# Unread TensorE products in front of five waits of each turn of a four-layer kernel

## The chip, the cores and the metric

The kernel runs on one core of one Trainium2 chip. The metric is the device time of one execution in microseconds, as the median of several runs. A profile of one execution comes with it; its span is the time from the first instruction to the last.

## What is computed

The reference is a stack of four residual layers on x of 8 x 512 x 256 (batch, tokens, features) in float32:

```python
x = x + mamba(layernorm(x))        # in_proj, conv, silu, x_proj, dt_proj, selective scan over 16 states, out_proj
x = x + attn_gated_mlp(layernorm(x))   # 16-head causal softmax attention that modulates a 1024-wide gated MLP
x = x + gla(layernorm(x))          # gated linear attention in chunks of 64, 4 heads
x = x + moe(layernorm(x))          # router over 32 experts, top 4, 96-wide experts
```

Every product is between float32 operands unless the kernel casts them.

## The kernel before

The batch is worked off in eight turns of 512 tokens. Each engine has one program, written by hand, and semaphores tie them together. A turn has two parts. `scan_part(turn)` is the first layer: transposes, the input products, the state scan in 32 units (VectorE lines 1399, 1367 and 1376; ScalarE line 1097 makes the decay; TensorE line 2047 adds a unit's two states by transposing products), then the output product. `rest_part(turn)` is the attention, the MLP and the linear attention. `rest_part(turn)` runs beside `scan_part(turn + 1)`: on each engine `weave` takes so many steps of the one and so many of the other, by a list `ORDER` that is fixed in the code. A step ends at a `yield`. So every engine issues in a fixed order, and a wait of one part also holds what is queued of the other. Router work of an older turn (`late_logits`, line 1979) goes along in the scan part. After the eighth turn the experts' blocks follow alone.

PSUM has eight banks: two for the scan part (ring A), four for the rest part (ring B), two (D) for attention outputs and the MLP's down product. `room(ring, turn, key)` waits until the reader of the bank's previous contents is done. A product with `start=True` overwrites.

The waits of TensorE that the change touches, by what comes behind them:

- the last scan unit (`unit == NU - 1`): waits for VectorE line 1376. Behind it stand the unit's own eight transposing products (line 2047), then the transposes `goT` of the rest part, then those of y (line 1923), then the output products (line 1949).
- `zn`, the first wait of `rest_part`: normed tokens from ScalarE line 1110. Behind it: `zT` transposes (line 1923), router logits (line 1979), q and k products (line 1936).
- behind the `nmT` transposes (row maxima): a wait for VectorE line 1550. Behind it: transposed scores `ST` (lines 2135 and 2138) into all four banks of ring B, which ScalarE line 1144 takes the exponential of, and the products with v (line 2148).
- `gn`: normed tokens from ScalarE line 987. Behind it: `nT` transposes, the products `low` (line 1936, 128*16) and `gk`, then q, k, v and gate products.
- `kd`: decayed keys from VectorE line 1614. Behind it: `kdT` transposes, `dS` products (line 1936, 64*128) and scan units.

`unread` is there before the change and is used in the last turn only, ahead of the scores:

```python
def unread(bank_, n, wide):
    for _ in range(n):
        if wide:
            t_.matmul(bank_[:, 0:SEQ], ident[:, :], chunk_starts[:, :], start=True, stop=True)
        else:
            t_.matmul(bank_[:, 0:SEQ], ident_b[:, :], ones_b[:, :].unsqueeze(1).broadcast_to([P, SEQ // P, P]), start=True, stop=True)
```

Of the kernel before, what the change touches and what calls it, by code (L numbers as in the profile page):

```python
# [25 lines left out]
BATCH, SEQ, HID = 8, 512, 256  # L26
# [113 lines left out]
NU = NPAIR * NCT  # L140
# [127 lines left out]
def rest_jobs():  # L268
    jobs = [("zT", c, "act") for c in range(NF)]
    jobs += [("q", i, "act") for i in range(NQT)] + [("k", i, "act") for i in range(NQT)]  # L270
    jobs += [("v", i, "act") for i in range(2)]
    jobs += [("S", u, "dve", 2) for u in range(NSU)] + [("nmT", i, "dve") for i in range(NQT)]
    jobs += [("ST", u, "act", HPT) for u in range(NTU)] + [("OT", i, "dve") for i in range(NQT)]
    jobs += [("oT", c, "act") for c in range(NF)] + [("mod", 0, "act"), ("hA", 0, "dve")]
    for f in range(NFT):
        jobs += [("gate", f, "act"), ("up", f, "dve")]
    jobs += [("nT", c, "act") for c in range(NF)]
    jobs += [("low", 0, "act"), ("gk", 0, "act"), ("gq", 0, "act"), ("gkey", 0, "act")]
    jobs += [("gv", i, "act") for i in range(2)] + [("gg", i, "act") for i in range(2)]
    jobs += [("kdT", 0, "act")]  # L280
    jobs += [("dS", c, "dve") for c in range(NCHUNK - 1)] + [("AT", t, "dve") for t in range(NT)]
    jobs += [("GO", t, "act") for t in range(NT)] + [("goT", c, "act") for c in range(NF)]
    jobs += [("gout", i, "dve") for i in range(2)]
    return [((job[0], job[1]), job[2], job[3] if len(job) > 3 else 1) for job in jobs]
# [17 lines left out]
def build(nc, counted, x, w, wt, mod_b, wo, g_gk2, g_norm, out):  # L302


    with ExitStack() as ctx:
# [6 lines left out]
        def sem(name):  # L312
            return ctx.enter_context(nc.semaphore(name))
# [161 lines left out]
        goT = xT  # L475
# [66 lines left out]
        B = Ring(sem, "rest_bank", bank[2:6], rest_jobs())  # L542
        D = bank[6:8]
# [3 lines left out]
        d_free = Signal(sem("d_free"), NT + 1, primed=True)  # L547
# [1349 lines left out]
        def _(pe):  # L1897
# [12 lines left out]
            def room(ring, turn, key):  # L1910

                for freed, value in ring.room(turn, key):
                    pe.wait_ge(freed, value)
# [39 lines left out]
# [9 lines that stand above are left out]
            def late_logits(turn, late, ring=A):  # L1962
                yield
                if late is None:
                    if turn:
                        pe.wait_ge(A.ready.sem, A.ready.at(turn, 0))
                    pe.sem_inc(A.ready.sem, NF + 1)
                    yield
                    yield
                    return  # L1970
                pe.wait_ge(ra.sem, ra.named(late, "mn"))
                yield from to_features(ring, turn, "mT", stage)
                yield
                pe.wait_ge(ring.freed_sem(("mT", 1)), ring.freed_at(turn, ("mT", 1)))
                room(ring, turn, ("rt", 0))
                b = ring.bank(("rt", 0))
                for t in range(NT):
                    for c in range(NF):
                        m = t_.matmul(b[:, t * EXPERTS:(t + 1) * EXPERTS], mT[:, c, t * P:(t + 1) * P], router[:, c],
                                      start=(c == 0), stop=(c == NF - 1))  # L1980
                filled(ring, m)
# [30 lines left out]
            def scan_part(turn, late):  # L2012
                yield from late_logits(turn, late)
                yield
                pe.wait_ge(sa.sem, sa.named(turn, "xn"))
                yield from to_features(A, turn, "T", xn)
                yield
                pe.wait_ge(A.freed_sem(("T", 1)), A.freed_at(turn, ("T", 1)))
                for n in range(2 * NCT):
                    yield  # L2020
                    product(A, turn, (("hid", "gate")[n // NCT], n % NCT),
                            [(m_in[:, c, n * P:(n + 1) * P], xnT[:, c]) for c in range(NF)])
                    yield
                yield from late_rank(turn, late)
                yield
                pe.wait_ge(sa.sem, sa.named(turn, "u"))
                yield from token_product(A, turn, "ssm", u, m_x, NSSM, NCT)
                yield
                pe.wait_ge(sv.sem, sv.named(turn, "ssm_n"))
                transposes(A, turn, ("dtT", 0), [(slice(t * P, (t + 1) * P), ssm[:, t, 0:DTRANK]) for t in range(NT)])  # L2030
                yield
                transposes(A, turn, ("bcT", 0), [(slice(t * P, (t + 1) * P), ssm[:, t, DTRANK:]) for t in range(NT)])
                yield
                pe.wait_ge(A.freed_sem(("dtT", 0)), A.freed_at(turn, ("dtT", 0)))
                for c in range(NCT):
                    if c == 2:
                        yield
                    product(A, turn, ("dtp", c), [(m_dt[:, c * P:(c + 1) * P], dtnT)])
                for unit in range(NU):
                    _, pair, c = unit_of(unit)  # L2040
                    yield
                    if pair == 0:
                        room(A, turn, ("yT", c))
                    pe.wait_ge(unit_done.sem, unit_done.at(turn, unit + 1))
                    for n in range(2):
                        for t in range(NT):
                            m = t_.matmul(A.bank(("yT", c))[:, t * P:(t + 1) * P], drive[:, unit % NDRIVE, n, t * P:(t + 1) * P], ident[:, :], is_transpose=True,  # L2047
                                          start=(pair == 0 and n == 0 and t == 0), stop=(pair == NPAIR - 1 and n == 1), skip_group_check=True)
                    m.then_inc(unit_summed.sem, 1)
                    if pair == NPAIR - 1:  # L2050
                        pe.wait_ge(unit_summed.sem, unit_summed.at(turn, unit + 1))
                        pe.sem_inc(A.ready.sem, 1)  # L2052
                        if c % 2:
                            for back in (c - 1, c):
                                yield
                                pe.wait_ge(A.freed_sem(("yT", back)), A.freed_at(turn, ("yT", back)))
                                transposes(A, turn, ("y", back), [(slice(t * P, (t + 1) * P), dtu[:, back, t * P:(t + 1) * P]) for t in range(NT)])
                yield
                pe.wait_ge(sv.sem, sv.named(turn, f"y{NCT - 1}"))
                yield from token_product(A, turn, "out", dtu, m_out, HID, NCT)  # L2060
                yield
# [19 lines left out]

            def rest_part(turn):
                yield
                pe.wait_ge(ra.sem, ra.named(turn, "zn"))
                yield from to_features(B, turn, "zT", zn)
                yield
# [36 lines left out]
                for i in range(NQT):  # L2123
                    yield
                    transposes(B, turn, ("nmT", i), [(slice(t * P, (t + 1) * P), nmax[:, t, i]) for t in range(NT)])
                yield
                pe.wait_ge(B.freed_sem(("nmT", NQT - 1)), B.freed_at(turn, ("nmT", NQT - 1)))
                for u in range(NTU + LAG):
                    if u < NTU:
# [36 lines left out]
                for f in range(NFT + 1):  # L2166
                    if f < NFT:
                        yield
                        mlp_tile(turn, f, hT, [(modb[:, f * P:(f + 1) * P], gmod)])
                    if f:  # L2170
                        yield
                        down(turn, f - 1, NT, f == 1, f == NFT)
                    yield
                pe.wait_ge(ra.sem, ra.named(turn, "gn"))
                yield from to_features(B, turn, "nT", nrm)
                yield
# [11 lines left out]
                yield  # L2188
                yield from token_product(B, turn, "gg", xT, g_g, GHV, NF)
                yield  # L2190
                pe.wait_ge(rv.sem, rv.named(turn, "kd"))
                transposes(B, turn, ("kdT", 0), [(slice(t * P, (t + 1) * P), e_kd[:, t * P:(t + 1) * P]) for t in range(NT)])
                yield
# [305 lines left out]
```

## Time and profile before

| | us |
|---|---|
| device time, median of 3 runs | 3018.92 (3018.33 to 3037.64) |
| span of the profiled execution | 2958.7 |
| TensorE busy | 2351.0 (79%) |
| VectorE busy | 2163.5 (73%) |
| ScalarE busy | 1383.5 (47%) |
| one turn in the steady state | 307.2 |

The profiled execution's span is 60.2 us below the median of the runs; no other time of that execution is shown. The time of a turn is the distance between two equal events of neighbouring turns (1066.87 and 1374.06 us). A float32 product appears in the trace as two matmul records, each with its own weight load; a float32 transpose likewise. Clocks are given as a share of full speed: 1.00 is 2.4 GHz, 0.50 is 1.2 GHz.

### The profile page before, as it was taken

To read this page: it belongs to the slowest core of one execution; us is meant where nothing else is said; L and a number is where in the kernel's file an instruction comes from. 1 tells how busy PE (TensorE), PEld (TensorE's weight loads), DVE (VectorE), ACT (ScalarE), POOL (GpSimd) and SP (SyncE) were. 2 spreads that over 40 slices of the span, in tenths; PEclk is the share of its full clock that TensorE was granted. 3 is DMA by queue.
4 is the path that set the end of the run, shared out by engine and by line. 5 is a ranking of instruction groups with operands and counts; after the bars stand their busy time and mean duration, and the time that the engine had idled before them with its cause. 6 is when DMAs were issued, how large, how long until landed. Compare 5 with 4: busy or idle time off the path is not lost. (4 is left out here: it accounts for less than half of the span.)

```text
span 2958.7 us, 36517 instructions
## 1 busy us (share of the span) xinstructions
PE 2351.0 (79%) x12305; PEld 1420.5 (48%) x12305; DVE 2163.5 (73%) x3017; ACT 1383.5 (47%) x2217; POOL 575.3 (19%) x569
## 2 busy tenths in 40 slices
PE   4448896889778977887788869787879688988991
PEld 2335354535453545444544545345535453556880
DVE  4993898489948894899669975998589852246666
ACT  5323654366535663566356634654465424143440
POOL 4000101120131013111311120212120230025661
PEclk8558897899889987998799979998999789988995
DMA  2320231023201321133113311231033182355757
GB/s 105 120 79 8 103 113 57 15 87 128 74 28 60 128 94 35 42 126 107 42 35 109 117 49 42 92 127 56 8 112 121 60 212 97 103 195 174 219 180 302
DMA packets 136229, 292.85 MB, mean 99 GB/s; under 512 B 14288, under 2 KB 79200, under 8 KB 135792
## 3 DMA queue, kind: packets, MB, share of 16 engines
q1 hardware_dynamic: 122224, 251.96, 26.2%
q0 software_dynamic: 13824, 38.55, 3.6%
q8 instruction: 104, 1.70, 0.2%
q14 instruction: 77, 0.63, 0.1%
HBM read 220.91 MB, written 69.54 MB: 98 GB/s over the span
## 5 line engine op out<-in xcount | busy, mean ns | idle before, releaser
L1367 DVE TENSOR_TENSOR_SCAN scan<-scan 128x1024 f32<-128x1024 f32 x256 | 585.9, 2289 | 34.4 <-ACT scan L1097 26.4
L2047 PE MATMUL bank<-ident,scan 128*128 128x128 f32 x2048 | 325.3, 315 | 168.9 <-DVE scan L1376 158.1
L1097 ACT ACTIVATE scan<-scan 128x511 f32<-128x511 f32 x512 | 337.2, 713 | 164.2 <-DVE scan L1367 163.5
L2047 PEld LDWEIGHTS bank<-ident,scan 128*128 128x128 f32 x2048 | 271.6, 162 | 260.1 <-DVE scan L1376 158.4
L1399 DVE TENSOR_TENSOR scan<-scan 128x1024 f32<-128x1024 f32 x256 | 310.5, 1213 | 29.5 <-PE bank L2047 28.5
L1376 DVE TENSOR_TENSOR scan<-scan 128x1024 f32<-128x1024 f32 x256 | 312.0, 1219 | 7.8 <-DVE rest L1579 7.5
L1936 PE MATMUL bank<-hT,wslot 128*128 128x512 f32 x512 | 246.9, 607 | 0.0
L1541 DVE TENSOR_REDUCE rest<-bank 128x2 f32<-128x1024 f32 (+3 forms) x176 | 196.5, 1126 | 66.5 <-PE bank L2118 63.5
L819 POOL DMA_INDIRECT rows_dram<-stage,slot_at x128 | 164.9, 1288 | 370.4 <-DVE scan L1367 313.1
L1144 ACT ACTIVATE rest<-bank 128x2048 f32<-128x2048 f32 (+3 forms) x128 | 158.2, 1236 | 146.7 <-PE bank L2138 146.6
L1936 PE MATMUL bank<-xT,scan 128*128 128x512 f32 (+1 forms) x352 | 185.0, 672 | 7.4 <-ACT xT L983 4.8
L2113 PE MATMUL bank<-rest 32*128 32x384 f32 (+3 forms) x1024 | 185.4, 464 | 2.3 <-DVE rest L1541 1.7
L1321 DVE SCALAR_TENSOR_TENSOR scan<-scan 128x512 f32<-128x512 f32 x96 | 71.9, 752 | 144.9 <-ACT scan L1033 142.4
L983 ACT ACTIVATE scan<-bank 128x512 f32<-128x512 f32 x112 | 65.2, 595 | 230.1 <-PEq L2052 89.5
L1936 PE MATMUL bank<-scan 128*128 128x512 f32 x320 | 153.2, 608 | 3.6 <-ACT scan L983 3.1
L797 POOL TENSOR_SCALAR rs<-mv 128x4 f32<-128x4 f32 x24 | 10.1, 421 | 691.9 <-DVE off L1300 691.9
L1936 PEld LDWEIGHTS bank<-hT,wslot 128*128 128x128 f32 x512 | 88.8, 189 | 115.4 <-issue 108.6
L1923 PE MATMUL bank<-ident,rest 128*128 128x128 f32 x352 | 57.8, 324 | 107.5 <-ACT rest L1110 52.6
L2135 PE MATMUL bank<-causal_t,ident_b 128*128 128x128 bf16 x512 | 54.8, 235 | 105.5 <-ACT rest L1144 67.7
L894 POOL DMA_INDIRECT y_dram<-rest,y_at x120 | 115.1, 959 | 60.6 <-DVE rest L1867 47.5
L2071 PE MATMUL bank<-wslot,rest 128*128 128x256 f32 x512 | 120.4, 380 | 1.0 <-PE bank L2047 0.2
L1163 ACT ACT_TABLE_LOAD x49 | 62.9, 1283 | 120.7 <-PE bank L1936 120.6
(341 smaller groups left out, 4231.2 us busy)
## 6 DMA issues: line engine op xcount, KB each, us to landing
scan<-bc_dram SPq DMA_DIRECT2D x256, 512.0 KB, 3.8
wslot<-wt SPq DMA_DIRECT2D x64, 384.0 KB, 3.5
rows_dram<-pad SPq DMA_DIRECT2D x32, 670.0 KB
scan<-y_dram SPq DMA_DIRECT2D x32, 512.0 KB, 10.1
rest<-rows_dram SPq DMA_DIRECT2D x108, 134.0 KB, 2.5
scan<-rows_dram SPq DMA_DIRECT2D x52, 134.0 KB, 2.7
scan<-wt SPq DMA_DIRECT2D x4, 1536.0 KB, 13.6
xa<-x SPq DMA_DIRECT2D x8, 512.0 KB, 3.8
```

What stands on the lines that cost most here:

```text
L819: g.indirect_dma_start(rows_dram, bass.IndirectOffsetOnAxis(ap=slot_at[:, j:j + 1], axis=0), stage[:, j % NT], None).then_inc(scattered.se ...
L894: g.indirect_dma_start(y_dram, bass.IndirectOffsetOnAxis(ap=y_at[:, b % NYA:b % NYA + 1], axis=0), y[:, n % y.shape[1]], None).then_inc(y_ ...
L1097: i = a.activation(decay[:, unit % 2, n, 1:], dt[:, c, 1:], ACT.Exp, scale=a_neg[:, c, 2 * pair + n:2 * pair + n + 1])
L1144: a.activation(probT[:, u % NPT, :, 0:SEQ - j * P], banks(("ST", u))[:, :, 0:SEQ - j * P], ACT.Exp)\
L1367: d.tensor_tensor_scan(flat, decay[:, unit % 2].rearrange("p n t -> p (n t)"), flat, 0.0, ALU.mult, ALU.add).then_inc(decay_used.sem, 1)
L1376: d.tensor_tensor(drive[:, unit % NDRIVE], drive[:, unit % NDRIVE], bc[:, load % 2, 1], ALU.mult).then_inc(unit_done.sem, 1)
L1399: d.tensor_tensor(drive[:, unit % NDRIVE], dtu[:, c].unsqueeze(1).broadcast_to([P, 2, SEQ]), bc[:, load % 2, 0], ALU.mult).then_inc(drive_ ...
L1541: d.tensor_reduce(nmax[:, t, heads, r].rearrange("p i r -> p r i"), banks(("S", u))[:, :, 0:n * width].rearrange("p r (i k) -> p r i k", i=n),
L1936: m = t_.matmul(b[0:rows, cols], lhsT, rhs, start=(i == 0), stop=(i == len(pairs) - 1))
L2047: m = t_.matmul(A.bank(("yT", c))[:, t * P:(t + 1) * P], drive[:, unit % NDRIVE, n, t * P:(t + 1) * P], ident[:, :], is_transpose=True, st ...
L2071: m = t_.matmul(D[t // 2][:, (t % 2) * HID:(t % 2 + 1) * HID], inner[:, f % 2, t * P:(t + 1) * P], slot[:, 2 * NF * P:], start=(first and ...
L2113: t_.matmul(b[:, k, at:at + width], qT[rows, i, t * P:(t + 1) * P], kT[rows, i, 0:width], start=(i == heads.start), stop=False, skip_group ...
```

## The change

In front of the five waits the program now waits for room in the bank that it overwrites next and issues 5, 6, 5, 7 and 5 float32 products of 128x512 (`ident` by `chunk_starts`) into it. Nothing reads them; the next real product or transpose in that bank overwrites them. They do not occur in every turn: `zn` has them in turns 1 to 6, `nmT`, `gn` and `kd` in turns 0 to 6, and the last scan unit in turns 2 to 7. The order of the rest is unchanged.

```diff
@@ scan_part, loop over units @@
                     if pair == 0:
                         room(A, turn, ("yT", c))
+                    if turn > 1 and unit == NU - 1:
+                        room(B, turn - 1, ("goT", 0))
+                        unread(B.bank(("goT", 0)), 5, True)
                     pe.wait_ge(unit_done.sem, unit_done.at(turn, unit + 1))
@@ rest_part @@
                 yield
+                if 1 <= turn < BATCH - 1:
+                    room(B, turn, ("zT", 0))
+                    unread(B.bank(("zT", 0)), 6, True)
                 pe.wait_ge(ra.sem, ra.named(turn, "zn"))
...
                 yield
+                if turn < BATCH - 1:
+                    pe.wait_ge(d_free.sem, d_free.at(turn, 0))
+                    unread(D[0], 5, True)
                 pe.wait_ge(B.freed_sem(("nmT", NQT - 1)), B.freed_at(turn, ("nmT", NQT - 1)))
...
                     yield
+                if turn < BATCH - 1:
+                    room(B, turn, ("nT", 0))
+                    unread(B.bank(("nT", 0)), 7, True)
                 pe.wait_ge(ra.sem, ra.named(turn, "gn"))
...
                 yield
+                if turn < BATCH - 1:
+                    room(B, turn, ("kdT", 0))
+                    unread(B.bank(("kdT", 0)), 5, True)
                 pe.wait_ge(rv.sem, rv.named(turn, "kd"))
```

## Rows read from the trace of the kernel before

**Rows 1.** Waits of TensorE over the whole span (us in total, times, longest).

```profile
PE bank L2047 <- DVE scan L1376: 158.1, 57, 22.6
PE bank L1923 <- ACT n_all L987: 53.6, 8, 7.6
PE bank L1923 <- ACT rest L1110: 52.6, 7, 8.6
PE bank L1923 <- DVE rest L1614: 42.9, 8, 6.0
PE bank L2135 <- DVE rest L1550: 37.8, 8, 5.5
```

**Rows 2.** Stretches of one turn: busy time (x), then TensorE's clock, DMA share, GB/s.

```profile
1066.80:1072.80 6.00, 5.25 (x12) 1.99 (x12) 4.82 (x5) 3.63 (x7) 3.83 (x2) 0.50 0.50 166
1094.00:1100.10 6.10, 5.41 (x19) 3.38 (x20) 4.86 (x4) 4.95 (x9) 0.00 (x0) 0.50 0.27 86
1130.00:1135.20 5.20, 0.00 (x0) 0.00 (x0) 2.44 (x6) 0.60 (x1) 4.70 (x3) 0.50 0.08 26
1135.20:1141.00 5.80, 5.47 (x25) 5.10 (x26) 2.20 (x3) 1.97 (x3) 4.58 (x5) 0.50 0.26 92
1141.00:1153.00 12.00, 11.77 (x57) 9.74 (x56) 7.33 (x19) 2.67 (x5) 6.33 (x7) 1.00 0.20 69
1160.20:1168.30 8.10, 8.02 (x28) 6.47 (x29) 2.72 (x13) 3.57 (x8) 1.40 (x3) 0.50 0.24 68
1245.30:1253.70 8.40, 6.34 (x32) 1.93 (x32) 8.26 (x7) 3.34 (x3) 3.24 (x2) 0.50 0.00 0
1300.00:1366.00 66.00, 65.70 (x253) 37.25 (x252) 63.01 (x54) 38.94 (x48) 1.14 (x1) 1.00 0.38 127
1366.50:1442.30 75.80, 48.49 (x254) 30.90 (x254) 66.17 (x73) 35.74 (x60) 17.31 (x10) 0.79 0.19 63
```

**Rows 3.** TensorE in order of time around the five waits of that turn.

```profile
1066.87 1.97 PE L1923 MATMUL bank<-ident,n_all 128*128 128x128 f32 x8 [7.61 <-ACT n_all L987]
1069.52 3.48 PE L1936 MATMUL bank<-xT,scan 128*16 128x512 f32 x4 [0.69 <-ACT xT L983]
...
1094.00 1.11 PE L1923 MATMUL bank<-ident,rest 128*128 128x128 f32 x4 [6.05 <-DVE rest L1614]
...
1135.23 1.97 PE L2047 MATMUL bank<-ident,scan 128*128 128x128 f32 x8 [5.23 <-DVE scan L1376]
1137.50 1.94 PE L1923 MATMUL bank<-ident,n_all 128*128 128x128 f32 x8 [0.30 <-PE bank L2047]
...
1160.28 1.97 PE L1923 MATMUL bank<-ident,rest 128*128 128x128 f32 x8 [7.33 <-ACT rest L1110]
1162.04 3.46 PE L1979 MATMUL bank<-scan 128*128 128x32 f32 x16
1165.31 8.60 PE L1936 MATMUL bank<-xT,scan 128*128 128x512 f32 x16
...
1245.88 2.09 PE L2138 MATMUL bank<-rest 32*128 32x512 f32 x8
...
1250.51 1.66 PE L2138 MATMUL bank<-rest 32*128 32x384 f32 x8
```

**Rows 4.** VectorE's waits for TensorE in that turn, in order of time.

```profile
1077.69 1.23 DVE L1399 TENSOR_TENSOR scan<-scan 128x1024 f32<-128x1024 f32 x1 [2.81 <-PE bank L2047]
...
1098.96 1.23 DVE L1399 TENSOR_TENSOR scan<-scan 128x1024 f32<-128x1024 f32 x1 [1.24 <-PE bank L2047]
...
1293.92 0.26 DVE L1556 RECIPROCAL prob_sum<-bank 128x16 f32<-128x16 f32 x1 [2.01 <-PE bank L1923]
```

**Rows 5.** The unread products of the last turn, in order of time.

```profile
2415.55 2.84 PE L1958 MATMUL bank<-chunk_starts,ident 128*128 128x512 f32 x6 [0.48 <-ACT rest L983]
```

**Rows 6.** The same kinds of work at full clock, in order of time.

```profile
1271.79 1.14 PE L2138 MATMUL bank<-rest 32*128 32x512 f32 x8
...
1299.11 1.89 PE L1936 MATMUL bank<-xT,wo_a 128*16 128x512 f32 x4 [0.74 <-ACT xT L983]
```

## The prediction

> **What bounds the kernel now.** I read the page first. TensorE is busy 79% of the span and VectorE 73%, so neither is the bound everywhere, and the question is which of them sets the end of each stretch. The list of TensorE's waits comes next [rows 1]: beside the wait for scan units, four groups stand out, each with seven or eight waits of nearly one length (53.6/8, 52.6/7, 42.9/8 and 37.8/8 us). They are the waits in front of `nT`, `zT`, `kdT` and `ST`, once a turn. In the turn that I follow they last 7.61, 7.33, 6.05 and, ahead of `ST`, about 5.5 us, and the wait of the last scan unit lasts 5.23 us [rows 1, 3]. The same five recur in each steady turn.
>
> The third view is the busy time in stretches with the granted clock [rows 2]. Behind each of the five waits TensorE works at 0.50, which is 1.2 GHz, for about 6 to 8 us, and in the dense MLP stretch it works at 1.00, 2.4 GHz. In every case the engine had been idle for 5 to 8 us just before. That is the cost that a change of this kind can touch: not the waits, which other engines end, but the slow work behind them.
>
> The fourth view is VectorE in order of time. In the MLP stretch both engines are nearly full (65.70 and 63.01 of 66.00 us), in the stretch behind it VectorE is (66.17 of 75.80) and TensorE is not (48.49) [rows 2]. There VectorE leads, and a faster TensorE pays only where VectorE waits for it: 2.81 us behind the `gn` wait, 1.24 us behind `kd`, 2.01 us at the end of attention [rows 4]. In the serial stretch around 1135 to 1175 and in the scores the chain runs through TensorE.
>
> **What the change adds.** Per turn 5 + 6 + 5 + 7 + 5 = 28 products, two matmul records each. Six such records took 2.84 us with the last one's latency [rows 5]; I take 0.43 us a record at full clock (1.89 us for four of 512 columns [rows 6], less the latency at the end) and 0.87 at 1.2 GHz (3.48 us for four [rows 3]). So seven products take 6.0 us, six 5.2, five 4.3 at full clock; the waits are 7.61, 7.33 and 6.05, 5.5, 5.23 us. At full clock all fit, with 0.9 to 2.2 us to spare. The room that they wait for is given long before by ScalarE or VectorE: the gate product of two MLP tiles earlier, the v product, the GO product, the output product of the turn before, the down product of the turn before. I cost the added waits at nothing; the releaser of each bank has worked before the wait starts, since TensorE had issued that bank's job at least one stage earlier. If that cover were gone, the products would start late and hold the real work behind them, at 0.43 us a record. Nothing else is queued differently; no DMA is issued by it.
>
> **`gn` wait, 7 turns.** Behind it eight transposes took 1.97 us and the four `low` records 3.48 us [rows 3]. At full clock four such records take 1.89 us [rows 6], a gain of 1.6. Of the transposes I count 0.8 (they would take about half, and ScalarE's copies stand between). The chain gains 2.4 us. VectorE waited 2.81 us for TensorE just behind it [rows 4], so it can take all of the 2.4. 7 x 2.4 = 16.8 us. Bounds: 0 (the clock falls anyway), 2.8 (the whole wait).
>
> **`kd` wait, 7 turns.** Four transposes (1.11 us) and a scan unit are in front of what VectorE waits for. Half of 1.11 and of a unit's 1.97 is 1.5 us, more than the wait of 1.24 us [rows 3, 4]. I take 1.24: 7 x 1.24 = 8.7 us. Bounds 0 and 1.24.
>
> **Wait ahead of `ST`, 7 turns.** The scores fill four banks, ScalarE empties them, and only then the next fill: a serial chain. The two fills behind the wait took 2.09 and 1.66 us at 1.2 GHz [rows 3]; 2.09 becomes 1.14 [rows 6], and by the same ratio 1.66 becomes 0.91. With the small products in front of them (some 0.2 each) that is 2.1 us. VectorE waits 2.01 us at the end of this chain [rows 4], so it follows. In turn 0 the products meet a shorter wait and a slow clock, which I count as no gain. 6 x 2.1 = 12.6 us. Bounds 0 and 2.1.
>
> **`zn` wait, 6 turns.** Behind it stand 1.97 + 3.46 us of transposes and router logits and then 16 records that took 8.60 us [rows 3]; at full clock these 16 take 16 x 0.43 = 6.9. The first two can't shrink to half, since ScalarE has to copy `zT` four times before q; from 1160.28 to the end of the 16 it is 13.6 us now and would be about 3.1 + 7.0 = 10.1 at best. Best case 3.5 us, worst (clock gone again right behind the transposes) 0.8. The spare time behind the unread products is the longest here, 2.1 us, so I take the middle, 2.1: 6 x 2.1 = 12.6 us. What follows to 1240 is dense on TensorE at full clock and passes the gain on.
>
> **Last scan unit, 6 turns.** This one differs: the clock is already at 0.50 when the wait starts, as 1130.00 to 1135.20 shows [rows 2]. Ten records at 0.87 would take 8.7 us in a wait of 5.23, an overrun of 3.5. But the clock came back within about 6 us once TensorE worked without a break [rows 2]; with 4 to 6 us of it slow, the products end 1.1 to 2.1 us late. In return the unit, `goT` and y transposes behind it (1.97, 1.94 and as much again [rows 3]) shrink by some 2.7 us. Net 0.7 us, 6 x 0.7 = 4.2 us. Bounds: -3.5 and +1.8.
>
> **Sum.** 16.8 + 8.7 + 12.6 + 12.6 + 4.2 = 54.9 us. The profiled span 2958.7 becomes 2903.8. The median stands 60.2 us above the span and keeps that: 3018.9 - 54.9 = 2964.0 us.
>
> **The rivals.**
>
> *The clock falls again.* 0.9 to 2.2 us of idleness remain in front of each real product. No row shows whether that much brings the clock down, so I can't exclude it. Then only the first microseconds of each stage are fast, and I count some 1.7 us a turn, 7 x 1.7 = 12 us: 3007 us. For it: the `zn` rest is long. Against: three of the spares are under 2 us. Chance 0.10. A sentence of the Trainium skill stands on its own here ("TensorE: Matmul & The Clock Gate", Part 4, PE-mode transpose): it says that the full clock does not engage for transposes. By it the transposes behind four of the five waits would lose the clock again and the outcome would be near this rival. The trace disagrees: between 1135.2 and 1141.0 TensorE did nearly nothing but transposes, at 0.50, and from 1141.0 it had 1.00 [rows 2].
>
> *VectorE keeps the gain.* In 1366 to 1442 it is busy 66.17 of 75.80 us [rows 2], and its waits for TensorE sum to 2.81 + 1.24 + 2.01 = 6.1 us a turn [rows 4]. If a wait for ScalarE or GpSimd takes the place of half of that and the serial stretch gives nothing, 7 x 3 = 21 us are left: 2998 us. Chance 0.12.
>
> *More than the five stretches.* Other short slow stretches lie in a turn. If they go too (about 3 us a turn) and `zn` gives its best, the sum is 55 + 21 + 8 = 84 us: 2935 us. Chance 0.05.
>
> *Slower: the unread products run at 1.2 GHz and hold the real work.* If the clock were already low at the start of each wait, they would take 12.2, 10.4 and three times 8.7 us against 7.61, 7.33, 6.05, 5.5 and 5.23: 4.6 x 7 + 3.1 x 6 + 2.7 x 7 + 3.2 x 7 + 3.5 x 6 = 113 us, 3132 us. It decides from the point where about half of the starts are slow. For it: the last unit starts slow. Against: the `gn` wait follows 66 us at 1.00 [rows 2], and the others follow dense work too. Chance 0.05.
>
> **How the numbers follow.** The forecast has 0.68, the others 0.10, 0.12, 0.05 and 0.05. About 1% (30 us) is what a measurement of this kernel can tell from no change. Faster by over 1% is the forecast and the better rival: 0.73. Within 1% are the two that keep 12 and 21 us, less a little: 0.21. Slower: 0.06. The range goes from the better rival's 2935, a little lower for the bounds of the other terms, to the 3007 of the falling clock: 2932 to 3007.
>
> **What would show it.** In the changed profile line 1958 should have 14 + 10 + 10 + 12 + 10 = 56 records in a steady turn, the waits of [rows 1] for lines 1110, 987, 1614 and 1550 should be down to 1 to 2 us each, and the granted clock should be 1.00 behind `gn`, `kd`, `zn` and the `ST` wait. The 3.48 us of `low` should read 1.89, the 8.60 us should read about 7.0. VectorE's wait of 2.81 us should be about 0.4, that of 1.24 gone. A turn should take 307.2 - 9 = 298 us. The prediction is wrong if the clock still reads 0.50 behind the waits, if new VectorE waits of 2 to 3 us for ScalarE or GpSimd appear, or if the unit behind the last unread products starts more than 2 us late.

## The result, and the profile after

| | before | after |
|---|---|---|
| device time, median of 17 runs each | 3028.94 us | 3042.15 us |
| ratio, with its 95% interval | | 1.0047 (1.0033 to 1.0062) |
| the five steady turns (1 to 5) | 307.4, then 307.2 us four times | 311.8, 315.3, 308.6, 306.0, 312.6 us |
| TensorE busy | 2351.0 us | 2553.0 us |
| mean granted clock | 0.870 | 0.884 |

The kernel became 0.47% slower, 13 us, which lies within the 1% that the prediction had called no change (chance 0.21); its forecast was 2964.0 us, 55 us faster. A turn was to take 298 us and takes 311 on average. The spans of the two profiled executions (2958.7 and 3043.7 us) must not be compared: behind the last turn's start every kernel of this study, the unchanged one too, takes either 543 to 548 us or 604 to 615 us, by the group of runs it was measured in, so what follows compares turns, and ratios within one group of runs. (This is the size of the 60.2 us between span and median of before, too.) Turns are counted from VectorE's line 1532, which starts once in each. Turn 0 grew as well, from 306.2 to 309.6 us, and turn 6 from 331.6 to 338.0: from the first of these starts to the last the profiled execution of after took 27.8 us more than that of before. That is twice the 13 us between the medians, and no run shows where the other half went, so the turns below tell where time is lost, not how much the median execution loses.

What the unread products were to do, they do. TensorE's list of waits, after (line waited at, releaser: us in total, times, longest):

```profile
PE bank L2050 <- DVE scan L1376: 141.8, 56, 22.6
...
PE bank L1923 <- ACT rest L1110: 21.7, 7, 8.6
...
PE bank L1923 <- DVE rest L1614: 12.8, 8, 1.8
PE bank L1923 <- ACT n_all L987: 11.9, 8, 1.6
```

The groups of 52.6, 42.9 and 53.6 us [rows 1] are down to 21.7, 12.8 and 11.9, which is 1.6 to 2.2 us for each in the turns; line 2047 is now 2050. The waits ahead of `ST` are down from 37.8 to 2.3 us. Behind the waits TensorE in order of time, after, with the clock 1.00 behind `gn`, `kd` and `ST`:

```profile
1079.82 1.09 PE L1923 MATMUL bank<-ident,n_all 128*128 128x128 f32 x8 [1.60 <-ACT n_all L987]
1082.00 1.89 PE L1936 MATMUL bank<-xT,scan 128*16 128x512 f32 x4 [1.09 <-ACT xT L983]
...
1104.90 0.66 PE L1923 MATMUL bank<-ident,rest 128*128 128x128 f32 x4 [1.76 <-DVE rest L1614]
...
1176.42 1.09 PE L1923 MATMUL bank<-ident,rest 128*128 128x128 f32 x8 [2.18 <-ACT rest L1110]
1177.35 2.08 PE L1979 MATMUL bank<-scan 128*128 128x32 f32 x16
1179.59 8.46 PE L1936 MATMUL bank<-xT,scan 128*128 128x512 f32 x16 [0.16 <-ACT hT L1117]
...
1259.82 1.14 PE L2147 MATMUL bank<-rest 32*128 32x512 f32 x8
```

`low` takes 1.89 us instead of 3.48 and the first `ST` fill 1.14 instead of 2.09, as forecast [rows 3, 6]. Only behind `zn` the clock falls again: it is 1.00 for the transposes and most of the logits (2.08 instead of 3.46), 0.50 from 1178.9 to 1182.3 and 1.00 again behind that, so the 16 records of q and k take 8.46 us. Before they took 8.60, with the clock at 0.50 until 1168.3 and 1.00 from there. From the first transpose to the end of the 16 it is 11.6 us here, 13.6 before [rows 3].

So why is a turn longer? VectorE's waits say where. VectorE's busy time in a turn stays the same (243.97 us before, 244.07 us for the changed kernel profiled again, below), so a turn grows or shrinks as VectorE's waits do. The list of VectorE's waits within one turn, before (1158.5 to 1465.7):

```profile
DVE scan L1321 <- ACT scan L1033: 18.5, 1, 18.5
...
DVE rest L1541 <- PE bank L2118: 7.3, 9, 2.9
...
DVE scan L1399 <- PE bank L2047: 4.0, 2, 2.8
...
DVE scan L1505 <- PE bank L1923: 3.6, 1, 3.6
...
DVE g_ss L1640 <- ACT hT L1216: 0.9, 1, 0.9
```

and within one turn after (1789.3 to 2101.7):

```profile
DVE scan L1321 <- ACT scan L1033: 17.2, 1, 17.2
DVE rest L1541 <- PE bank L2124: 9.9, 10, 5.0
DVE g_ss L1640 <- ACT hT L1216: 8.2, 2, 4.6
...
DVE scan L1505 <- PE bank L1923: 1.6, 1, 1.6
...
DVE scan L1399 <- PE bank L2050: 0.7, 1, 0.7
```

Line 1399 is the scan unit behind `gn` and `kd`, line 1505 reads the output product's banks behind the last scan unit, line 1321 is behind the serial stretch with `zn`. These three gained 3.3, 2.0 and 1.3 us. Line 1541 reads the attention scores, line 1640 sums the squares of `go`, the output of the linear attention: they lost 2.6 and 7.3 us. No edit touches either. The stage whose products line 1640 waits for, through ScalarE, is called GO: 78 records of narrow products. TensorE in order of time just ahead of it and at its start, after:

```profile
1122.35 0.65 PE L2222 MATMUL bank<-rest 128*64 128x256 f32 x4 [1.78 <-DVE rest L1623]
1124.62 1.97 PE L2050 MATMUL bank<-ident,scan 128*128 128x128 f32 x8 [1.62 <-DVE scan L1376]
1126.52 1.11 PE L2238 MATMUL bank<-rest 64*64 64x64 f32 x8
1127.56 1.11 PE L2236 MATMUL bank<-rest 128*64 128x256 f32 x2
```

The same before (there 2207, 2047, 2223 and 2221):

```profile
1110.69 3.10 PE L2207 MATMUL bank<-rest 128*64 128x256 f32 x12
1114.95 1.09 PE L2047 MATMUL bank<-ident,scan 128*128 128x128 f32 x8 [1.15 <-DVE scan L1376]
1116.03 0.65 PE L2223 MATMUL bank<-rest 64*64 64x64 f32 x8
1116.61 0.65 PE L2221 MATMUL bank<-rest 128*64 128x256 f32 x2
```

The products of GO run at 1.2 GHz now, and not for a moment. The busy time in stretches (start, end, length, TensorE, its weight load, VectorE, ScalarE, GpSimd, then TensorE's granted clock), first after, then before:

```profile
1124.30:1141.40 17.10, 16.78 (x81) 10.87 (x82) 10.92 (x14) 3.19 (x8) 0.00 (x0) 0.50 0.01 1
```

```profile
1116.00:1126.00 10.00, 9.97 (x87) 6.50 (x86) 9.48 (x11) 3.19 (x8) 0.00 (x0) 1.00 0.00 0
```

TensorE is busy 16.78 of 17.10 us (with 16 transposing records of scan units among the 81), and the clock is back only at 1141.3, with 14 of GO's 78 records left. From the first record of GO to the last it is 16.4 us, 9.9 before. In the five steady turns 56, 62, 78, 10 and 64 of GO's 78 records are slow (at 0.50 for over half of their time), before none. In time that is line 1640's extra wait: 5.9, 7.3, 8.4, 1.5 and 7.3 us. In four of the five turns the scores (line 2119) also lose the clock in the middle of dense work (four records in 2.08 us, the same four in 1.13 a little later), and line 1541 waits 2.4 to 2.6 us longer.

Why does GO meet a low clock? The rows ahead of it say what came first. Before, the AT products (line 2207, the stage ahead of GO) ran with the clock at 0.50, from 1106.9 to 1113.7; TensorE was late itself, waited for VectorE only once in the last 6 us, for 1.15 us, and began GO at 1.00. After, the clock was 1.00 from 1110.6 to 1124.2; TensorE was done sooner, waited twice, 1.78 and 1.62 us, and the clock fell at 1124.2, in the second wait. This pair of waits, 1.8 and 1.6 us, both within the 6 us ahead of GO, stands in every turn with 60 or more slow records, in all kernels below that add nothing around GO, and in no turn of before. It isn't enough by itself: with the same pair only 9 or 10 records are slow in most turns of `only_kd`, and with 1.6 and 1.6 us none in turn 0 of after again.

The difference from before, VectorE's waits turn by turn:

| line, what it stands for | turn 1 | 2 | 3 | 4 | 5 | mean |
|---|---|---|---|---|---|---|
| 1399, behind `gn` and `kd` | -2.7 | -3.3 | -2.6 | -3.3 | -3.3 | -3.0 |
| 1505, last scan unit | -2.0 | -0.8 | -2.0 | -0.9 | -2.0 | -1.5 |
| 1321, serial stretch with `zn` | -0.5 | +1.3 | -2.1 | -0.4 | -1.3 | -0.6 |
| 1640, GO | +5.9 | +7.3 | +8.4 | +1.5 | +7.3 | +6.1 |
| 1541, scores | +2.5 | +2.6 | 0 | +2.4 | +2.6 | +2.0 |

The five means give +3.0; other waits bring it to the +3.6 us that a turn has grown (310.8 on average against 307.2).

### The profile page after: what moved, and what is told of

Read it like the earlier page. It is cut to its first block and busy times, and to the rows that moved or that the text cites. A ratio compares the mean times of both kernels' runs of the same rounds, so it can differ in the third digit from the quotient of the medians.

```text
span 3043.7 us, 37257 instructions
## 1 busy us (share of the span) xinstructions
PE 2553.0 (84%) x12675; PEld 1507.9 (50%) x12675; DVE 2168.0 (71%) x3017; ACT 1380.2 (45%) x2217; POOL 585.1 (19%) x569
## 5 line engine op out<-in xcount | busy, mean ns | idle before, releaser
L1399 DVE TENSOR_TENSOR scan<-scan 128x1024 f32<-128x1024 f32 x256 | 310.8, 1214 | 8.1 <-PE bank L2050 7.1
L819 POOL DMA_INDIRECT rows_dram<-stage,slot_at x128 | 173.9, 1359 | 365.5 <-DVE scan L1367 308.6
L2119 PE MATMUL bank<-rest 32*128 32x384 f32 (+3 forms) x1024 | 202.0, 498 | 2.3 <-DVE rest L1541 1.7
L1936 PE MATMUL bank<-xT,scan 128*128 128x512 f32 (+1 forms) x352 | 178.2, 652 | 10.4 <-ACT xT L983 7.6
L1958 PE MATMUL bank<-chunk_starts,ident 128*128 128x512 f32 x376 | 177.6, 623 | 1.4 <-ACT rest L983 0.5
L797 POOL TENSOR_SCALAR rs<-mv 128x4 f32<-128x4 f32 x24 | 10.1, 422 | 680.7 <-DVE off L1300 680.7
L1949 PE MATMUL bank<-scan,xT 128*128 128x256 f32 x512 | 117.0, 381 | 0.3
## 6 DMA issues: line engine op xcount, KB each, us to landing
scan<-y_dram SPq DMA_DIRECT2D x32, 512.0 KB, 10.1
```

The lines of the kernel that those rows point to most:

```text
L819: g.indirect_dma_start(rows_dram, bass.IndirectOffsetOnAxis(ap=slot_at[:, j:j + 1], axis=0), stage[:, j % NT], None).then_inc(scattered.se ...
L1399: d.tensor_tensor(drive[:, unit % NDRIVE], dtu[:, c].unsqueeze(1).broadcast_to([P, 2, SEQ]), bc[:, load % 2, 0], ALU.mult).then_inc(drive_ ...
L1936: m = t_.matmul(b[0:rows, cols], lhsT, rhs, start=(i == 0), stop=(i == len(pairs) - 1))
L2119: t_.matmul(b[:, k, at:at + width], qT[rows, i, t * P:(t + 1) * P], kT[rows, i, 0:width], start=(i == heads.start), stop=False, skip_group ...
```

## The experiments

The theory to be tested: the unread products pay what they were to pay, and a turn gets longer because TensorE's clock is now low in other stretches, GO above all. Rivals: one of the five edits is itself harmful where it stands (its products or its added wait hold something), or the loss comes from some delay that has nothing to do with the clock. "On X" below is the kernel that the edit is made to.

**Both kernels again.** No edit.

> The unchanged kernel before, to see whether its profile repeats. Theory A (alignment): the profile with a span of 2958.7 us and turns of exactly 307.2 us is one fortunate way in which the clock's falls line up with the work; this profile will show a span of 3015 to 3035 us, turns of 310 to 318 us, and the clock at 0.50 during the products of lines 2221 and 2223 in most turns. Theory B (the change itself costs time): the profile repeats at 2955 to 2965 us with 307.2 us a turn, and the 85 us between the two profiles is the change's doing. Ratio to the kernel before 1.000.

> The changed kernel once more. Theory A: span 3030 to 3050 us, behind the gn, kd and ST waits the clock is at 1.00 again, and it is at 0.50 during lines 2236 and 2238 (the products that were 2221 and 2223) in most of the turns, at other places than in the first profile. Theory B: the same span, with the loss at the unread products themselves, that is waits behind them that start late. Ratio 1.003 to 1.006 in both.

Before: ratio 0.9996 (0.9977 to 1.0015), turns 307.4, 307.2, 307.2, 307.2, 307.2. After: 1.0054 (1.0024 to 1.0084), turns 302.3, 312.5 and then 314.0 three times. So before repeats to 0.2 us a turn, against theory A of its expectation (one fortunate profile). After is repeated in its ratio, but not in its single turns: the same kernel settled in another sequence, one which repeats as exactly as that of before. In the turn that it reached at 302.3 no narrow product was slow; in those at 314.0, 64 of 78 were. The stretch of one whole turn, after again:

```profile
1160.20:1474.30 314.10, 282.47 (x1407) 160.70 (x1407) 244.07 (x290) 160.39 (x238) 54.37 (x45) 0.92 0.23 75
```

and before:

```profile
1158.50:1465.70 307.20, 254.09 (x1351) 147.04 (x1351) 243.97 (x290) 160.48 (x237) 54.37 (x45) 0.89 0.23 76
```

The mean clock is higher (0.92) and the turn 7 us longer: a mean hides where the slow part lies.

**One edit at a time.** On before, each the lines of the change at its place and nothing else: `only_gn`, `only_kd`, `only_zn`, `only_st` (ahead of `ST`), `only_unit` (last scan unit).

```diff
+                if 1 <= turn < BATCH - 1:          # only_zn; the others likewise
+                    room(B, turn, ("zT", 0))
+                    unread(B.bank(("zT", 0)), 6, True)
```

> Only the seven unread products ahead of gn. By the prediction's own term the gain is 2.4 us in each of 7 turns, ratio 0.9945. Theory A: the four low records take 1.89 us and VectorE's wait behind them goes, but the work behind shifts against the clock and gives some of it back: 0.995 to 1.000. Theory B (unread products hold real work): 1.000 to 1.003.

> Only the five unread products ahead of kd. By the prediction's term the gain is 1.24 us a turn, ratio 0.997. Theory A: full clock behind kd, but then the 2.4 us wait of line 2207 lets it fall and the products of lines 2221 and 2223, which stay slow once they start slow, take 16 instead of 10 us: 3 to 6 us lost in some turns, 1.000 to 1.008. Theory B: 1.000 to 1.003.

> Only the six unread products ahead of zn, turns 1 to 6. The prediction's term is 2.1 us a turn, ratio 0.996, best case 3.5 us, 0.993. Theory A (2.2 us of idleness remain and the 16 router records of 32 columns follow): the clock falls right behind the wait, the logits run at 0.50 in most turns, and the gain is under 1 us a turn, 0.998 to 1.000; a shift against the clock may take more than that back in the narrow products, up to 1.012.

> Only the five unread products ahead of ST, turns 0 to 6. The prediction's term is 2.1 us a turn, ratio 0.996. Theory A: the first two fills are faster by 2.1 us, but TensorE then waits about 2 us for scan unit 0, whose VectorE instruction ended only 0.15 us before TensorE took it: no gain, 0.999 to 1.001, unless the narrow products meet a low clock.

> Only the five unread products ahead of the last scan unit, turns 2 to 7. The prediction's term is a gain of 0.7 us a turn (bounds -3.5 and +1.8). Theory A: they begin at 0.50 and end 0.5 to 2 us late, y and goT transposes take half: within 1 us a turn either way, a turn of 306 to 308.5 us, ratio 0.997 to 1.003, if the shift does not cool another stretch.

| kernel | ratio (95%) | steady turns, us | slow GO records of 78 |
|---|---|---|---|
| only_gn | 1.0128 (1.0102 to 1.0154) | 306.8, then 314.0 four times | 0, then 61 |
| only_kd | 1.0006 (0.9991 to 1.0020) | 317.0, 307.3, 307.2, 307.2, 307.2 | 54, 10, 9, 9, 9 |
| only_zn | 1.0277 (1.0242 to 1.0312) | 320.7, then 320.8 four times | 65 each |
| only_st | 0.9998 (0.9978 to 1.0017) | 307.2, 307.1, 307.2, 307.2, 307.2 | 0 |
| only_unit | 1.0139 (1.0110 to 1.0168) | 306.3, 319.3, 315.6, 306.9, 319.5 | 0, 64, 9, 0, 64 |

Three single edits cost more than all five together, so they don't add up; all three lie outside everything that was expected of them (at most 1.003, 1.012 and 1.003). In the turns of `only_gn` and `only_zn` the loss is not where the edit stands. VectorE's waits in a turn of `only_zn`:

```profile
DVE scan L1321 <- ACT scan L1033: 17.9, 1, 17.9
DVE rest L1541 <- PE bank L2121: 9.9, 10, 4.4
DVE g_ss L1640 <- ACT hT L1216: 8.3, 2, 4.6
DVE scan L1399 <- PE bank L2047: 7.6, 2, 6.4
```

Against before: 0.6 us gained at its own place; lost 2.6 (scores), 7.4 (GO) and 3.6 us (the unit behind `gn`, which waits 6.4 instead of 2.8). The waits before and after the edit's own place show no loss from it, against the rival that the edit does harm where it stands. `only_gn` gained 0.7 us at line 1399 and lost 7.2 at GO: even its own term was not paid, since `low` took 3.3 us in these turns and 1.89 only in the first two. `only_unit`, in its turn of 315.6 us, gained 1.1 us at line 1505 and lost 3.7 behind `gn`, 2.6 in the scores and 1.5 at GO. `only_kd` did exactly what was forecast for it (line 1399: -1.2 us), and lost 1.6 us with nine slow records of GO: a turn of 307.2.

`only_st` is another case. The fills ran at full clock, the turn did not move. TensorE in order of time, `only_st`:

```profile
1246.29 1.14 PE L2141 MATMUL bank<-rest 32*128 32x512 f32 x8
...
1249.76 0.93 PE L2141 MATMUL bank<-rest 32*128 32x384 f32 x8
...
1256.36 1.06 PE L2047 MATMUL bank<-ident,scan 128*128 128x128 f32 x8 [1.40 <-DVE scan L1376]
```

TensorE won 1.3 us and then waits 1.40 us for a scan unit of VectorE, which ended at 1256.21; the products start 0.15 us behind it. Before, they started at 1255.76, also 0.15 us behind VectorE's end (1255.61), with no wait in the row. So there was nothing to be had in this place, not 2.1 us. And VectorE's wait at the end of attention (line 1556, 2.01 us [rows 4]), which was to go, became 3.5 us in this turn, as line 1367 waits 1.8 us less for ScalarE.

**Holding the clock in GO.** Six unread products around the AT products, which stand just ahead of GO, where the two waits are; they are called the GO products below:

```diff
+                    if turn < BATCH - 1 and t in (0, NT - 1):     # ahead of AT
+                        pe.wait_ge(d_free.sem, d_free.at(turn + 1, 0))
+                        unread(D[0], 2 if t == 0 else 2, True)
...
+                    if turn < BATCH - 1 and t == NT - 1:          # behind AT
+                        unread(D[0], 2, True)
```

On after (`after_go`), on before with the `gn` edit (`gn_go`), on before with `zn` at 8 instead of 6 (`zn8_go`), and on before alone (`before_go`).

> The changed kernel with the same six unread products around AT. Theory A: the narrow products run at 1.00, a turn takes 300 to 307 us in place of 314.0, ratio to before 0.980 to 1.000, and 0.98 to 0.99 to the changed kernel. Rival (unread products as such cost time): ratio 1.006 or more.

> The gn products, and with them six more unread products a turn around the AT products (two ahead of the first, two ahead of the last, two behind the last, in bank D[0]), so that the clock is full when the narrow products of the last linear attention stage (lines 2221 and 2223 of before) begin. With the gn products alone these ran at 0.50 in 61 of 78 records a turn, a turn took 314.0 us and the kernel was 1.3% slower. Theory A (the loss is only the clock in the narrow products): they run at 1.00 in every turn, a turn takes 307.2 us or less (304 to 307), ratio 0.990 to 1.000. Rival (unread products as such cost time, through their length or the banks): with 13 a turn the loss is as before or grows, a turn stays at 314 us or more, ratio 1.012 to 1.020.

> Eight unread products ahead of zn (not six) and the six around AT, none at the other four waits. With six ahead of zn alone a turn took 320.8 us, 13.6 us more than before. Theory A: with 0.5 us of idleness left instead of 2.2 the logits behind zn run at 1.00, the narrow products too, and a turn takes 302 to 307.2 us, ratio 0.985 to 1.000. Rival (the products ahead of zn themselves cost the 13.6 us): a turn still takes 315 us or more.

> The kernel before with only the six unread products around AT. The narrow products are at 1.00 there already, so theory A expects no gain: a turn of 307.2 us, ratio 0.998 to 1.002. The rival (a product in an idle stretch gives time by itself or costs time by itself) expects a turn that moves by over 1 us either way.

| kernel | ratio (95%) | steady turns, us |
|---|---|---|
| after_go | 0.9908 (0.9881 to 0.9935) | 299.4, 302.4, 305.2, 302.3, 305.2 |
| gn_go | 0.9984 (0.9967 to 1.0002) | 313.1, 307.2, 307.8, 307.0, 307.1 |
| zn8_go | 0.9963 (0.9944 to 0.9983) | 305.6, 304.0, 303.8, 308.4, 305.9 |
| before_go | 1.0006 (0.9973 to 1.0039) | 314.1, then 314.0 four times |

In all four the two waits ahead of GO are gone (none of over 0.1 us in its last 7 us), and no record of GO is at 0.50. `after_go` turns after's loss of 0.5% into a gain of 0.9%, with the five edits unchanged. A turn is 7.9 us shorter than in after (302.9 on average), and 6.0 of them are line 1640's wait: this is the evidence that the loss was mainly GO's clock and not the edits' own products or waits. In its turn of 305.2 line 1399 has its -3.3 and line 1505 its -2.0 us; the scores still lose 2.6.

`before_go` shows that this is no simple remedy, and it is not the turn of 307.2 us that was expected. The kernel that had no slow GO record was given products that nothing needed, and its ten runs fall in two groups, 2958.8 to 2968.3 (five) and 2999.7 to 3005.7 (five), beside 2957.2 to 2975.8 for before. The ratio in the table leaves out three of the upper group; the median of all ten is 2984.0 us, 0.6% above before's. The profile is of the slower kind, turns of 314.0 us. VectorE's waits there: GO +0, but scores +2.6 and `gn` +3.7. VectorE in order of time, `before_go`:

```profile
1724.36 1.23 DVE L1399 TENSOR_TENSOR scan<-scan 128x1024 f32<-128x1024 f32 x1 [6.47 <-PE bank L2047]
```

where before it is 2.81 [rows 4]. The stretch in front of it, `before_go`:

```profile
1707.00:1724.10 17.10, 12.87 (x27) 5.63 (x28) 9.71 (x7) 9.89 (x17) 6.43 (x4) 0.50 0.30 88
```

The `gn` wait ends at 1709.9, so the clock is at 0.50 for 14 us behind it; in before it was so for 6 us [rows 2].

`gn_go` gives nothing, although its GO is fast. TensorE in order of time, `gn_go`:

```profile
1997.75 1.09 PE L1923 MATMUL bank<-ident,n_all 128*128 128x128 f32 x8 [1.59 <-ACT n_all L987]
1999.93 3.46 PE L1936 MATMUL bank<-xT,scan 128*16 128x512 f32 x4 [1.09 <-ACT xT L983]
```

The same seven products, the same wait of 1.6 us behind them and the same 1.09 us of transposes as in after, but here `low` takes 3.46 us and there 1.89. So the clock falls in one kernel and not in the other behind the same idle times, 1.6 and 1.1 us. In four of the five steady turns of `gn_go` `low` took 3.2 to 3.6 us and line 1399 gained 0.4 to 0.8 us; in the one where it took 1.89 it gained 2.1.

`zn8_go` shows what the length of the rest is worth behind `zn`. TensorE in order of time:

```profile
1156.56 2.74 PE L1958 MATMUL bank<-chunk_starts,ident 128*128 128x512 f32 x6
1159.75 1.09 PE L1923 MATMUL bank<-ident,rest 128*128 128x128 f32 x8 [0.46 <-ACT rest L1110]
1160.68 1.87 PE L1979 MATMUL bank<-scan 128*128 128x32 f32 x16
1162.92 7.13 PE L1936 MATMUL bank<-xT,scan 128*128 128x512 f32 x16 [0.37 <-ACT hT L1117]
```

With eight products 0.46 us of the wait are left instead of 2.18, and the clock holds: 10.3 us from 1159.75 to the end of the 16 records, against 11.6 after. Line 1321 waits 15.3 us instead of 18.5, 3.2 us gained, near the prediction's best case of 3.5. The turns are only 1.7 us shorter on average (305.5): line 1541 waits 1.1 to 2.8 us longer in two of them and line 1399 3.7 in one.

**One disturbance, once.** If a short delay of another engine, made once, costs more than itself, and the cost lies in the same places, then the clock's position and not the unread products makes the loss. `kick_v`: on before, VectorE repeats one statistics instruction five times, 2.3 us in all, once, just ahead of line 1532 of turn 1, so that the delay itself counts to turn 0. `kick_p`: on before, the six GO products in turn 0 alone.

```diff
...
+                if isinstance(turn, int) and turn == 1:
+                    for k in range(5):
+                        d.bn_stats(stats[:, 0], xa[:, 0]).then_inc(held, 1)
+                        dve.wait_ge(held, k + 1)
```

> The kernel before without any added product: VectorE repeats one statistics instruction five times, once, at the start of rest_part of turn 1, some 2.5 us in all. Theory A (a turn settles into a repeating pattern of work and clock, and an edit can move it from one pattern to another): the turns behind it are either 307.2 us again within a turn or two, or stay at another length such as 314.0; in the second case the ratio is 1.01 or more though only 2.5 us were added. Rival (each product or delay costs what it costs): every turn but one is 307.2 us, ratio 1.001.

> The kernel before with the six unread products around AT in turn 0 only. With them in every turn the runs fell into two groups, at 2959 to 2968 and at 3000 to 3006 us, and the profile of the slower kind had turns of 314.0 us with the narrow products at 1.00. Theory A: the six products of turn 0 are enough to choose the pattern, so the runs fall into the same two groups, or a part of them, 40 us apart, and a profile of the slower kind has turns of 314.0 us from turn 1 to 6. Rival (the products cost time where they stand): all runs within the spread of before, 2955 to 2976 us, ratio 1.000.

`kick_v`: 1.0081 (1.0050 to 1.0111), turn 0 takes 308.6 instead of 306.2 us, which is the delay itself, and the next ones 321.9, 307.4, 307.3, 307.2, 307.2, with 65 slow records of GO in the first of these and none in the others. VectorE's waits in the turn behind the delay (line numbers here are up to five higher than before's):

```profile
DVE scan L1322 <- ACT scan L1034: 19.2, 1, 19.2
DVE rest L1546 <- PE bank L2123: 9.9, 10, 4.3
DVE g_ss L1645 <- ACT hT L1217: 8.3, 2, 4.6
DVE scan L1400 <- PE bank L2052: 7.6, 2, 6.4
```

9.9, 8.3 and 7.6 us: the very sizes of `only_zn`. A delay of 2.3 us, in a kernel without any unread product in these turns, cost 14.7 us on top of itself, and then before's turn of 307.2 us came back by itself. So before's turn is stable against one push; an edit that is in every turn can change it for good. `kick_p` tells less: 1.0027 (1.0007 to 1.0047), turns 307.3 and then 307.2, only turn 0 longer (312.2 against 306.2 us), so the expected 314.0 us do not appear. But the profile is of the faster runs (five at 3017 to 3028 us, seven at 3034 to 3040); how the slower ones go is not shown.

**All of it together.** `full`, on after: the GO products; `zn` 8, `gn` 8, `kd` 6, `ST` 6; two also ahead of the last scan unit but one; one within the scores, where they lost the clock.

```diff
-                    if turn > 1 and unit == NU - 1:
+                    if turn > 1 and unit >= NU - 2:
                         room(B, turn - 1, ("goT", 0))
-                        unread(B.bank(("goT", 0)), 5, True)
+                        unread(B.bank(("goT", 0)), 5 if unit == NU - 1 else 2, True)
...
+                    elif u == 14:
+                        unread(b[:, 0], 1, True)
```

> The changed kernel with the six unread products around AT, with more ahead of the waits so that less idleness is left (zn 8, gn 8, kd 6, ST 6), two ahead of the wait of the last scan unit but one, and one in the scores (ahead of the fifteenth unit). Theory A (the clock alone; each of the losses seen so far is a stretch that met a low clock): logits, narrow products and scores run at 1.00 in all turns, a turn takes 296 to 301 us against 307.2 before, ratio 0.972 to 0.985. Rival (the longer rows of unread products now overrun and hold the work behind them): a turn takes 303 us or more, ratio 0.988 or more.

2924.03 us beside 2966.44 for before: 0.9853 (0.9825 to 0.9881), the fastest kernel of the study. Turns 302.0, 300.7, 300.9, 297.5, 302.4, 300.7 on average, at the edge of what was expected (296 to 301). VectorE's waits in one turn of `full`:

```profile
DVE scan L1321 <- ACT scan L1033: 15.3, 1, 15.3
DVE rest L1541 <- PE bank L2126: 8.2, 10, 3.2
...
DVE scan L1505 <- PE bank L1923: 1.6, 1, 1.6
...
DVE g_ss L1640 <- ACT hT L1216: 1.0, 1, 1.0
...
DVE scan L1399 <- PE bank L2050: 0.7, 1, 0.7
```

Against before: -3.2 (`zn`), -2.0 (last unit), -3.3 (`gn`, `kd`), GO +0.1, scores +0.9, and +1.5 in line 1556 at the end of attention. That is 6.5 us a turn on average of the 8.5 that the prediction's terms add up to, and 42.4 of its 54.9 us in all, once the clock is held where the edits had put it at risk. The longer row ahead of `ST` overruns: in four of the five turns the real work starts 1.1 to 1.2 us late there, so the rival of this run is right in part.

## Why the prediction was wrong

- **What bounds the kernel**: right. The waits, the slow work behind them, and the places where VectorE waits for TensorE were read as they are.
- **`gn`, 2.4, and `kd`, 1.24 us a turn**: right in after. Line 1399's waits of 2.8 and 1.2 us became one of 0.7, so 3.3 of the 3.6 forecast. But `gn` alone did not pay: line 1399 gained 0.7 us a turn in `only_gn` and 0.4 to 0.8 in four of five turns of `gn_go`, since the clock had fallen by the time of `low`.
- **`ST`, 2.1 us**: wrong. The step was "VectorE waits 2.01 us at the end of this chain, so it follows". What it left out is TensorE's next partner: before, TensorE took the scan unit as soon as VectorE gave it, so a faster chain only waits. `only_st` measured 0.
- **`zn`, 2.1 us**: mis-sized. Line 1321 gained 0.6 us on average in after and in `only_zn`. The working's best case, 10.1 us, was met (10.3) when two more products closed the wait.
- **Last unit, 0.7 us**: mis-sized the other way. Line 1505 gained 2.0 us in three turns of after and 0.8 or 0.9 in two. In these two the unread products ended late and the real work started 1.4 and 1.2 us behind time, as the prediction had reckoned (1.1 to 2.1 us).
- **The added waits cost nothing**: right. In after every row of unread products starts within 0.5 us of the end of the product before it.
- **The sum, 54.9 us**: here is the step that failed. By VectorE's waits the edits brought 3.0 + 1.5 + 0.6 = 5.1 us a turn; GO and the scores took 6.1 + 2.0 = 8.1. The sum took each stretch by itself and left the clock of all others as it was, a term of exactly 0. What the runs showed in its place: with a faster stage ahead of it TensorE waits 1.8 and 1.6 us just before GO, and GO then meets a clock of 0.50, +6.1 us a turn. No number of before stood behind the zero: the trace of before shows GO's 10.0 us at 1.00 but never what GO does when it meets a clock of 0.50.
- **The rivals**: "the clock falls again" looked for it in the transposes behind each wait and priced it as a lost gain, not as a loss elsewhere. Its "three of the spares are under 2 us" should be four. The slower rival had another mechanism, late real work; the runs show only the 1.2 to 1.4 us ahead of the last unit in two of five turns and 0.2 to 0.3 us ahead of `ST` in four. The range of 2932 to 3007 us did not hold 3042. The turn of 298 us took off 9 us; the terms of one steady turn add up to 8.5.
- **The base**: the 60.2 us between span and median is real for the runs shown and absent in other groups of runs (2970 and 2966 us for before). It has no part in the error, as the ratio shows.

The Trainium skill ("TensorE: Matmul & The Clock Gate", Part 1, HAM oscillation) says that a wait recurring in a loop makes the clock fall and come back each time round. The trace agrees: behind the `gn` wait of 7.6 us, `low` took 3.5 to 3.6 us in each of the seven turns of before, and 1.89 in the last one, where the clock was full.

What stays open: why the same edit leads to 314.0 us at one time and to turns between 306 and 315 at another, and why the same two waits ahead of GO make 10 slow records at one time and 65 at another. The runs show where the clock is low, what TensorE did just before, and what it costs, not the rule by which it lands there. Nor was it found what makes the last part 60 us longer in some groups of runs. The Trainium skill (the same page, Part 1, What's actually happening) says that the chip watches TensorE's activity on a clock that runs free of the kernel, so that one and the same kernel can meet it differently from run to run. The two sequences of turns of after would fit that; no run here shows the cause.

## What to carry to other kernels

When an edit touches the clock, price the stretches that it does not touch as well: for each stretch that is fast now, ask what it would cost at half the clock, and whether TensorE will now reach it after a wait that was not there, and put that into the range on the slow side (here 7.4 + 2.6 + 3.6 = 13.6 us a turn, by which `only_zn` grew). Read where the next releaser stands, to the tenth of a microsecond, before counting a faster chain as a gain. And treat exactly repeating turns as one pattern of several: test an edit alone and together with the others, since neither adds up.

## What the runs showed of the hardware that was not expected

- A stage made faster can cost the next one its clock: with the AT products at 0.50 TensorE waited once, 1.15 us, and GO ran at 1.00; with them at 1.00 it waited 1.78 and 1.62 us and GO ran at 0.50, 16.4 instead of 9.9 us. With both waits filled it ran at 1.00 again.
- Dense work does not always bring the clock back soon: around GO 81 records kept TensorE busy for 16.78 of 17.10 us before the clock rose, while behind 5.8 us of little but transposes it was at 1.00 in before (1135.2 to 1141.0 [rows 2]). GO's products use 64 rows or 64 columns of the array. The scores, products of 32 rows, lost the clock in the middle of dense work (2.08 us for four records that take 1.13).
- The same idle times around the `gn` transposes, 1.6 and 1.1 us, went with a fallen clock in `gn_go` and not in after; behind `zn` the clock fell after 2.18 us and held after 0.46.
- A pipeline of five engines with this clock settles, in most of these kernels, in a turn that repeats to 0.1 us, of 307.2, 314.0 or 320.8 us, 6.8 us apart. A delay of 2.3 us, once, cost 14.7 on top of itself.
